# Gathers a block earlier in two expert stages, their first transfers issued during routing, and one group of four tiles at the head of an attention

## The reference

```python
# layer 0 (F = 704); layer 3 is the same with F = 512 and its own names
probs = softmax(xn @ router_w); w, idx = top_k(probs, 2); w = w / sum(w)
one_hot = jax.nn.one_hot(idx, 8)
expert_w = einsum('btke,btk->bte', one_hot, w)
acts = silu(einsum('bted,edf->btef', dispatched, gate_proj)) * einsum('bted,edf->btef', dispatched, up_proj)
y = einsum('bted,bte->btd', einsum('btef,efd->bted', acts, down_proj), expert_w)
x = x + y
# layer 1, attention: exp feature maps of keys, values and queries, 64 context rows, 16 heads
attn = softmax(einsum('nqhd,nkhd->nhqk', fm(q), fm(k)) / 16)
x = x + einsum('nhql,nlhd->nqhd', attn, fm(v)).reshape(N, S, -1) @ fc_w.T + fc_b
```

## Time and profile before

| | us |
|---|---|
| median of 3 runs (1800.82 to 1808.09) | 1805.71 |
| profiled execution | 1800.69 |
| its span, first to last instruction | 1798.8 |

### The profile page before, as it was taken

The page is one execution under the profiler, slowest core; times in us unless marked ns, Lnnn a source line. Parts: engine busy times, 40 slices in busy tenths (PEclk is TensorE's granted clock), DMA queues, the critical chain, the costliest instruction groups (busy, mean ns, idle before and its releaser), DMA issues. The chain is left out here.

```text
span 1798.8 us, 33336 instructions
## 1 busy us (share of the span) xinstructions
PE 1550.2 (86%) x11830; PEld 1155.5 (64%) x11831; DVE 958.4 (53%) x2462; ACT 487.2 (27%) x1029; POOL 486.0 (27%) x594
## 2 busy tenths in 40 slices
PE   5887999999979986999979899578897888988885
PEld 3653899999858742455444566346665654878785
DVE  4455244444359866766556333689885464222221
ACT  2331111011067531455621122223322431000000
POOL 0101344444400001111102343422120102455543
PEclk9998999999969998999999999788998998999998
DMA  4108677777510017244115133200000025666665
GB/s 142 40 8 277 221 226 223 218 212 222 154 50 2 2 36 194 61 108 111 52 32 170 50 88 82 62 24 13 1 1 1 2 62 189 206 200 201 200 182 140
DMA packets 128641, 200.84 MB, mean 112 GB/s; under 512 B 20368, under 2 KB 77968, under 8 KB 128336
## 3 DMA queue, kind: packets, MB, share of 16 engines
q1 hardware_dynamic: 107696, 169.65, 29.3%
q0 software_dynamic: 20832, 29.68, 8.4%
HBM read 166.21 MB, written 35.16 MB: 112 GB/s over the span
## 5 line engine op out<-in xcount | busy, mean ns | idle before, releaser
L1528 DVE TENSOR_REDUCE l1a_nm<-l1a_sc 128x1 f32<-128x512 f32 (+3 forms) x256 | 107.1, 482 | 53.7 <-PE l1a_sc L1664 53.7
L2271 PEld LDWEIGHTS e0b_gp<-e0b_xT,e0b_wgu 128*128 128x128 f32 x936 | 110.5, 192 | 4.2 <-issue 1.5
L2271 PE MATMUL e0b_gp<-e0b_xT,e0b_wgu 128*128 128x128 f32 x936 | 111.0, 275 | 1.9 <-DVE e0b_hT L2350 1.4
L2331 ACT ACTIVATE e0b_sg<-e0b_gp 128x640 f32<-128x640 f32 x78 | 33.5, 481 | 270.9 <-PE e0b_gp L2271 270.9
L2242 POOL DMA_INDIRECT y_sum<-e0b_yb,e_token x39 | 63.5, 1628 | 145.6 <-DVE e0b_yb L2358 142.5
L2271 PE MATMUL e0b_up<-e0b_xT,e0b_wgu 128*128 128x128 f32 x780 | 93.5, 275 | 0.0
L2242 POOL DMA_INDIRECT y_sum<-e3b_yb,e_token x39 | 63.0, 1617 | 102.2 <-DVE e3b_yb L2358 99.3
L2271 PEld LDWEIGHTS e0b_up<-e0b_xT,e0b_wgu 128*128 128x128 f32 x780 | 90.2, 192 | 0.0
L2331 ACT ACTIVATE e3b_sg<-e3b_gp 128x512 f32<-128x512 f32 x39 | 23.3, 597 | 236.2 <-PE e3b_gp L2271 236.2
L2271 PE MATMUL e3b_up<-e3b_xT,e3b_wgu 128*128 128x128 f32 x624 | 80.3, 285 | 0.0
L2271 PEld LDWEIGHTS e3b_gp<-e3b_xT,e3b_wgu 128*128 128x128 f32 x624 | 75.6, 192 | 3.5 <-issue 0.9
(11 more groups left out here) (619 smaller groups left out, 3755.9 us busy)
## 6 DMA issues: line engine op xcount, KB each, us to landing
e3b_wgu<-in_L_ffn_W SPq DMA_DIRECT2D x78, 512.0 KB, 4.6
e0b_wgu<-in_L_ffn_gate_proj SPq DMA_DIRECT2D x39, 704.0 KB, 4.3
e0b_wgu<-in_L_ffn_up_proj SPq DMA_DIRECT2D x39, 704.0 KB, 5.6
x_rows<-xn SPq DMA_DIRECT2D x3, 2048.0 KB, 8.6
l_parts<-l1p_split SPq DMA_DIRECT2D x16, 384.0 KB, 3.1
l_stack_k<-l_parts SPq DMA_DIRECT2D x48, 128.0 KB, 2.7
l_stack_q<-l_parts SPq DMA_DIRECT2D x48, 128.0 KB, 3.0
y_slots<-e1b_yb SPq DMA_DIRECT2D x38, 128.0 KB
```

The source lines that it names most:

```text
L1528: nc.vector.tensor_reduce(nm[:, g % 2, q, i:i + 1], sc[q], AX_X, ALU.max, negate=True).then_inc(max_done, 1)
L2271: last = nc.tensor.matmul(dst[:, f, :], wgu[j][:, k, at + f * P:at + (f + 1) * P], xT[j][:, k, :], start=(k == 0), stop=(k == KC - 1))
L2331: last = nc.scalar.activation(sg[rows, chunks, :], gp[rows, chunks, :], ACT.Silu)
```

## The change

It has four parts.

1. In `blocks`, GpSimd's order becomes gather n, store n-4, weights n-2 (before: gather n, store n-3, weights n-1). The conditions on which each waits stay as they were.
2. The buffers xb (both) and wgu0, and the semaphores of the weights, move into the plan, so they exist during routing. At the end of `route` GpSimd waits for `pair` and `token` and for x_rows, and gathers the rows of blocks 0 and 1. SyncE loads the gate and up weights of block 0 once step 20 is reached, ahead of the last down weights in e0 and ahead of w_pairs in both stages. TensorE gets 16 fillers behind the token table's products, and in `blocks` 4 fillers in place of 30.
3. For e0 `homes` becomes inner, xn, xnT: the half chunk now lies in xnT, so GpSimd clears it at the start of routing without a wait; the load into xnT waits for the clearing, the loads into xn for the stores of x_rows.
4. In a1 the first two groups of two tiles become one of four. The second root and its table load ahead of the first query exponential go. On VectorE the statistics of the four tiles and the additions onto vz 0 and 1 come ahead of `invert(0)`, those onto vz 2 and 3 behind it.

```diff
-        GROUPS = [(0, 2), (2, 4)] + [(b * TB, (b + 1) * TB) for b in range(1, B)]
+        GROUPS = [(b * TB, (b + 1) * TB) for b in range(B)]
...
                     copy_rows(0)
-                    roots(1)
                     act.preload_act_table(ACT.Exp)
...
-                        for g in range(2, len(GROUPS)):
+                        for g in range(1, len(GROUPS)):
...
-                    for b in range(B):
+                    for t in range(TB):
+                        count(t)
+                    for t in range(TB):
+                        aggregate(t)
+                    for b in range(2):
                         dve.wait_ge(v_made, b // 2 * 2 + 2)
                         nc.vector.tensor_tensor(vz[:, b, :] ...
-                    for g in range(2):
-                        lo, hi = GROUPS[g]
-                        for t in range(lo, hi):
-                            count(t)
-                        for t in range(lo, hi):
-                            aggregate(t)
-                        invert(g)
+                    invert(0)
+                    for b in range(2, B):
+                        dve.wait_ge(v_made, b // 2 * 2 + 2)
+                        nc.vector.tensor_tensor(vz[:, b, :] ...
...
-            homes = [inner, xnT, xn]
+            homes = [inner, xn, xnT] if self.FC > 4 else [inner, xnT]
...
+        def load_gate_up(self, sp, owner, n, j):
+
+            e = sp.value_load(owner[0:1, bass.ds(n, 1)], min_val=0, max_val=self.E - 1)
+            for at, m in ((0, self.w_gate), (self.F, self.w_up)):
+                sp.dma_start(self.wgu[j][:, :, at:at + self.F], m[e].rearrange("(k p) f -> p k f", p=P)).then_inc(self.gu_in[j], 16)
...
                     last.then_inc(token_made, 1)
+                    if plan is not None:
+                        stay_busy(idle[:], 16)
...
                     sp.dma_start(x_rows[0:T * P, :].rearrange("(t p) d -> p t d", p=P), xn[:]).then_inc(sent, 16)
                     if plan is not None:
-                        for dst, source in plan.late[0]:
+                        if plan.LEFT:
+                            sp.dma_start(x_rows[T * P:, :].rearrange("(t p) d -> p t d", p=P), xn[:, 0:2, :]).then_inc(sent, 16)
+                            sp.wait_ge(left_cleared, 1)
+                        for dst, source in plan.late[-1]:
                             sp.dma_start(dst, source).then_inc(plan.kept, 16)
-                        if len(plan.late) > 1:
-                            sp.dma_start(x_rows[T * P:, :].rearrange("(t p) d -> p t d", p=P), xn[:, 0:2, :]).then_inc(sent, 16)
+                        sp.wait_ge(step, 20)
+                        plan.load_gate_up(sp, owner, 0, 0)
+                        if plan.LEFT:
                             sp.wait_ge(sent, 32)
-                            sp.wait_ge(left_cleared, 1)
-                            for dst, source in plan.late[1]:
+                            for dst, source in plan.late[0]:
                                 sp.dma_start(dst, source).then_inc(plan.kept, 16)
                         sp.wait_ge(tabled, 1)
...
                     if plan is not None and plan.LEFT:
-                        pool.wait_ge(sent, 32)
                         plan.clear_left(left_cleared)
...
+                    if plan is not None:
+                        pool.wait_ge(routed, 2)
+                        pool.wait_ge(sent, 32 if plan.LEFT else 16)
+                        for n in range(2):
+                            pool.indirect_dma_start(plan.xb[n][:], None, x_rows, bass.IndirectOffsetOnAxis(ap=token[:, n:n + 1], axis=0))\
+                                .then_inc(rows_in[n], 16)
...
-                        nc.vector.tensor_copy(token[:], row_f[:])
+                        nc.vector.tensor_copy(token[:], row_f[:]).then_inc(routed, 1)
...
-                    load_gate_up(0, 0)
-                    load_gate_up(1, 1)
+                    plan.load_gate_up(sp, owner, 1, 1)
                     step(0, 0)
...
-                    fetch(0)
-                    fetch(1)
                     fetch_weight(0)
                     fetch_weight(1)
                     pool.wait_ge(plan.start_written, 16 * len(plan.start))
                     for n in range(2, NB):
                         fetch(n)
-                        if n >= 3:
-                            send(n - 3)
-                            fetch_weight(n - 1)
-                    send(NB - 3)
-                    fetch_weight(NB - 1)
-                    send(NB - 2)
-                    send(NB - 1)
+                        if n >= 4:
+                            send(n - 4)
+                            fetch_weight(n - 2)
+                    for n in range(NB - 4, NB):
+                        send(n)
+                        if n + 2 < NB:
+                            fetch_weight(n + 2)
...
-                    stay_busy(gp[:, 0:4, :].rearrange("p f c -> p (f c)"), 30)
+                    stay_busy(gp[:, 0:4, :].rearrange("p f c -> p (f c)"), 4)
```

49 lines of the change are left out of this document (25 added, 24 removed).

## The result

The changed kernel has a median of **1760.75 us** (1755.03 to 1764.26) against 1803.26 (1799.31 to 1808.09) for the kernel before in the same session, a ratio of 0.976 [0.973, 0.980]. Run again in another session it had 1761.52, ratio 0.977 [0.975, 0.979]. The forecast was 1752, its range 1741 to 1772: the direction and the range were right, and of 51.3 us expected 42.5 and 40.6 came. Both medians lie just above the forecast's own range of 1744 to 1760 and near its rival (b), "the heads give nothing", which stood at 1763. The profiled execution took 1757.95 us, span 1756.0.

What follows compares the result with a forecast made beforehand. e0 was taken as bound by TensorE's work, e3 by TensorE waiting for gathers queued behind stores on GpSimd. Gains 37.5 + 7.9 + 3.0 + 2.9 = 51.3 us from 1800.69 gave 1749.4; median put at 1752, range 1741 to 1772.

Steps and rivals of the forecast that it cites:

- rival (b): Both stage heads gain nothing: fillers at the lower level end last, w_pairs lands behind 1.4 MB more; 1763 us, chance 0.07.
- The steady part of e3: Third expert stage's blocks: gathers issued one block earlier end TensorE's stalls, period 5.52 us; gain 37.5 us, bounds 30 and 39.
- The 1.4 taken off for loads and stores: In e3's steady part, deducted from 38.9 us because weights and stores fit only barely, giving 37.5.
- Both margins of 0.1 and 0.2 us: In e3's blocks, time in hand at the worst landings: 0.2 us for weights, 0.1 for stores.
- a: In e3's blocks gathers land in time, but weights or stores are late next: period about 5.9, 1767 us, chance 0.13.
- d: In e3's blocks accumulating stores land later and their chain sets the period, slower than before: 1820 us, chance 0.04.
- The attention: In a1 between the expert stages: one table load and root fewer, first shift 1.3 us earlier; gain 2.9 us, bounds 0 and 4.
- The head of e0: Routing and start of the first block stage: earlier numbers and earlier stage start; gain 7.9 us, bounds 5 and 11.
- the 2.7 for the clearing: Head of e0: without the clearing's wait the token table's products start at 170.2 instead of 172.9, gain 2.7 us.
- the 4.7: Head of e0: upper bound of the clearing's gain if GpSimd and VectorE kept their separate times, products at 168.2.
- The stage start: Head of e0: w_pairs lands at about 177.4 and two gathers are issued by 176.5, so the stage starts at about 177.9.
- The head of e3: Start of the third expert stage: later boundary but 4 fillers after it, gate product earlier; gain 3.0 us, bounds 0 and 5.

Runs made afterwards that it cites:

- order_only: Kernel before with only GpSimd's new order in the blocks (store n-4, weights n-2): 1765.83 us, ratio 0.979.
- attention_only: Kernel before with only a1's one group of four tiles and its order of additions onto vz: 1798.84 us, ratio 0.998.
- no_heads: Kernel before with GpSimd's new order and a1's one group of four tiles, nothing of the two heads: 1758.34 us, ratio 0.977.
- heads_only: Changed kernel with GpSimd's old order and the old groups of roots, leaving only the edits of both heads: 1798.41 us, ratio 0.998.
- extra_gate: Changed kernel with one more 512 KB load per block in e3, read by nobody; e3's first weights also wait for x_rows: 1788.0 us, ratio 0.990.
- fill24: Changed kernel with 24 instead of 16 fillers behind the token table's products in both block stages: 1754.63 us, ratio 0.973.
- xn_moved: Changed kernel with e0's last down weights loaded in the block stage, TensorE's wait for them moved to the first down product, and 22 fillers: 1756.46 us, ratio 0.974.
- late_xn: Changed kernel with e0's last down weights (2.1 MB) loaded in the block stage behind the second block's weights, not in routing: 1763.23 us, ratio 0.978.
- gathers0: Changed kernel with the first two gathers issued in the block stage again, ahead of the weight columns: 1771.59 us, ratio 0.982.
- experiment 5: Changed kernel with only the first gather issued during routing, the second ahead of the weight columns in the block stage: 1760.12 us, ratio 0.977.
- gathers1: Changed kernel with only the first gather issued during routing, the second in the block stage: 1760.12 us, ratio 0.977.
- xn_token: Changed kernel with e0's last down weights issued in routing behind w_pairs once the token is there, and 22 fillers: 1758.04 us, ratio 0.975.

## Why the prediction was nearly right, and where the missing part is

The forecast's largest term was right and carried the number into the range; the two heads, 10.9 of the 51.3 us, gave nothing that the medians show. That is what rival (b) had said, at a chance of 0.07, though not for its first reason: the 16 fillers did not end last. The table counts from VectorE's first instruction of routing, so that an earlier or later arrival drops out (us; "2nd" and "3rd" are the starts of those gate products, "steady" is from the third to the last; the names are those of the experiments, "before" and "changed" the two kernels, "after_again" the repeat):

```
                e0: token  boundary  2nd    3rd     e3: boundary  3rd    steady
before              25.64  28.13     44.21  52.01       23.20     43.46  237.90
order_only          25.83  28.23     44.30  52.10       23.22     43.31  198.91
attention_only      25.65  28.23     44.24  52.03       23.22     44.25  235.35
no_heads            25.69  28.18     44.30  52.09       23.22     44.97  200.72
changed             22.40  28.93     38.80  46.59       27.67     43.74  199.27
after_again         22.29  29.15     40.63  48.42       27.71     44.08  199.22
heads_only          22.91  30.87     42.37  50.17       27.64     43.05  234.67
extra_gate (e0)     22.90  30.34     42.72  50.52
fill24              22.92  30.92     40.80  48.59       27.65     40.95  199.11
xn_moved            22.34  27.27     35.87  46.25       28.41     41.66  199.01
```

**The steady part of e3: right.** 37.5 was forecast. The means of "steady" are 236.0 over three profiles with the old order (before, attention_only, heads_only) and 199.5 over order_only, no_heads, changed and after_again, 36.4 less, and order_only measured 36.4 by its median. The 38.9 worked out from one execution was 2.5 too much; 1.9 of that is that this execution, 237.90, was longer than the mean of the three. The 1.4 taken off for loads and stores was put there for another reason, so that 37.5 came so near is in part luck. The gather's margin was forecast at 3.5 us; from its issue to its use are now 8.5, and its landing took up to 5.5 before. Both margins of 0.1 and 0.2 us held (rivals a and d): the stores waited for y, and behind the third block the gate products' weight loads sat idle for 0.8 us in all from 1540 to 1736.

**The attention: right, a little small.** 2.9 forecast; a1 took 137.8 to 138.0 us in three profiles with two groups and 134.1 on average in attention_only, no_heads, changed and after_again: 3.7. The median of attention_only, 3.4 below, agrees, with an interval that reaches 1.000.

**The head of e0: 7.9 forecast, 3.1 measured** (third gate product 52.06 on average in four profiles with the old head, 48.9 in four with the new, 1.5 to 5.5 apart). Of its terms, the 2.7 for the clearing was right, token 2.7 to 3.5 us earlier. place_hot and the numbers took 5.53 and 6.39 side by side, 7.24 from GpSimd's start to the table's products. By themselves they take 4.49 and 2.43, 6.92 together, and side by side both were done 6.62 us after the first began, so hardly anything overlapped and the 4.7 was not to be had. By the Trainium skill (SBUF — State Buffer, Who interferes with whom) a VectorE instruction with two inputs in SBUF contends with a GpSimd instruction that reads SBUF; the trace agrees. Two terms failed:
- *The stage start.* It was put at 177.9, 26.9 after the start of routing. It came 28.9 to 30.9 after it, later than with the old head. Without the 2.1 MB ahead of w_pairs it comes at 27.3 (late_xn 27.28, xn_moved 27.27). The estimate shared out 9.4 MB evenly at the 356 GB/s of one 10 us window and got 26.4 us; up to the boundary 294 GB/s were moved, and the last packet of w_pairs came at 178.40, 181.38 and 181.83 in three profiles, 27.4, 28.0 and 29.9 after the start of routing. Part of that is its own issue: SyncE spent 163.05 to 169.36 on issuing the two xn loads, and w_pairs went out at 169.47, in late_xn at 163.50. And a second holder of the boundary had been left out altogether, GpSimd's drain: the forecast counted the gathers' issue to 176.5, not their landing. In gathers0, with no gather in routing, e0's boundary (179.38) stood 0.97 behind the last packet of w_pairs (178.41); by that distance the drain cost 0.5 us or less in e0, and the queue of loads is most of the miss there.
- *The clock.* The gate product was costed at its old duration, 2.94. It took 4.27 to 5.49.

**The head of e3: 3.0 forecast, 0.4 measured** (third gate product 44.0 on average in four profiles with the old head, 43.31 to 44.97, and 43.6 in changed, after_again and heads_only, 43.05 to 44.08: no more than the scatter). The boundary (forecast 2.6 to 5.6 after the old one) came 4.5 later and the first gate product 29.4 after the start of routing, 4.0 earlier than before: up to there the forecast held, though the fillers and issues that it named were not what held the boundary: the drain did. Then 2.9 us went to the lower clock (6.82 from first to second gate product, 3.90 before). What the 30 fillers had covered was that clock: they were still running when it rose, before the first gate product, and the forecast had not costed their removal, though it had the lower level of the fillers in its own rows. The rest went to the idle time ahead of the third gate product, by the kernel's waits for the third block's weights, whose load is issued when the first up product is done: 1.13 to 2.09 us in these three profiles, 0.33 to 2.15 with the old head. That wait differs from one execution to the next and is not the edit's alone.

**The sum** of what was measured is 36.4 + 3.7 + 3.1 + 0.4 = 43.6. Routing itself began 150.6 to 151.0 us after the start in the four profiles with the old head and 150.9 to 153.4, 151.8 on average, in ten with a new one; what that 1 us is was not tried and stays open. With it 42.6 are left, beside 42.5 and 40.6 by the medians. The stretch from a1's end to e3's token, untouched in all of them, took 876.2 to 886.8 us: single executions differ by more than the two heads are worth, and the profiled one after was a lucky one in e0. But the stretch averages 879.9 in the four profiles with the old head (876.2 to 882.6) and 883.5 in the ten with a new one (879.9 to 886.8). Whether that is chance, or a price of the new heads that is paid outside them, no run separates; it would be as large as what the heads gain at their own places.

## What to carry to other kernels

Moving GpSimd's gathers ahead of a block's end did not make them free: its drain held the end until they had landed (0.4 to 0.6 us after the last packet), so either place such an issue early enough to land by then or issue only what the first step needs. When a shared queue of loads is on the path, a rate read over one busy window is too high for the whole: here 356 GB/s against 294. When fillers or idle waits are removed from a head, cost what they covered, here the clock of the next products. Judge an edit of a few microseconds by the distance from a mark just ahead of it, over several executions, and not by one profile's absolute times.

## What was unexpected in the hardware

The drain, as shown under 5. And the clock at the heads: the level of the first gate product, 1.2 or 2.4 GHz, went with how long TensorE had been idle ahead of the stage's 4 fillers, in all of these:

```
idle, us   first gate product, us
0.30       2.05  e3 fill24          (2.05 at the upper level)
0.37       2.94  e0 xn_moved        (2.94 at the upper level)
0.85       2.05  e3 extra_gate
1.08       2.05  e3 gathers1
1.65       2.94  e0 late_xn
2.45       3.78  e3 changed
3.31       4.27  e0 changed
3.39       5.32  e0 xn_token
3.52       5.49  e0 after_again
```

Up to 1.65 us of idle time left the clock at 1.00; with 2.45 and more it fell to 0.50 for some us, in these nine during the fillers or behind them and not during the idle time. In e0 of extra_gate (idle 5.12, product 5.49) it had fallen while TensorE was still idle. Idle time behind the fillers counts as well: in e3 of gathers0 only 0.30 us stood ahead of them, but 5.23 between them and the first turning, and the product took 3.78. In extra_gate 33 of the 39 gate products of e3 also took 2.05 us in place of 1.95 at a granted clock of 1.00, while the DMA engines were busy for 0.95 of the time; the cause was not tried.
